# A two-layer graph network behind graph attention: the mix in float32 on four 64x64 blocks of the array, loop written out

## What is computed

```python
u = einsum('bid,bjd->bij', h, h) / sqrt(384)
a = softmax(u, -1)
delta = a * adj
attn = delta / (delta.sum(-1, keepdims=True) + 1e-10)
hl, hs, hr = h @ wl.T + b_l, h @ ws.T + b_s, h @ wr.T + b_r
ctx = (attn * upper) @ hl + diagonal(attn)[..., None] * hs + (attn * lower) @ hr
h = relu((ctx - mean(ctx)) / sqrt(var(ctx) + 1e-12) * g + beta)
```

## Time and profile before

| | us |
|---|---|
| median of 3 runs | 1378.46 (1377.25 to 1379.92) |
| the profiled execution | 1381.73 |
| its span | 1380.0 |
| TensorE busy | 1313.9 |
| VectorE busy | 1057.1 |
| ScalarE busy | 757.1 |
| GpSimd busy | 597.1 |

### The profile page before, as it was taken

One profiled execution on the slowest core, in us unless ns is written; L12 is line 12 of the kernel. 1 busy time (PEld: TensorE's weight loads), 2 busy tenths in 40 slices (PEclk: granted clock), 3 DMA queues, 4 the chain that ended last, 5 costly groups with the idle time before them and its releaser, 6 DMA issues.

```text
span 1380.0 us, 37486 instructions
## 1 busy us (share of the span) xinstructions
PE 1313.9 (95%) x13568; PEld 1289.9 (93%) x13568; DVE 1057.1 (77%) x2665; ACT 757.1 (55%) x1579; POOL 597.1 (43%) x656
## 2 busy tenths in 40 slices
PE   3799999999999999999999999999999999999895
PEld 3799999999999999999999999999999999999884
DVE  3358877878877888887787887788888778787765
ACT  4355555565555565555555555556555556555553
POOL 1344444444444444444444445444444444444432
PEclk9799999999999999999999999999999999999997
DMA  7210111110011111011111011111101111101000
GB/s 243 78 40 2 51 51 52 52 50 19 30 50 50 50 50 40 9 50 50 50 50 50 19 31 50 50 50 50 39 11 50 50 50 50 50 15 26 25 13 24
DMA packets 49445, 62.74 MB, mean 45 GB/s; under 512 B 14320, under 2 KB 35952, under 8 KB 49392
## 3 DMA queue, kind: packets, MB, share of 16 engines
q1 hardware_dynamic: 49392, 62.03, 14.7%
HBM read 36.44 MB, written 12.58 MB: 36 GB/s over the span
## 4 chain that ended last, share of the span: by engine, by line
PE 94%; DMA 2%; issue 1%; DVE 1%; ACT 1%; POOL 0%; SPq 0%; POOLq 0%; ACTq 0%
PE bank L315 26%; PE bank L317 25%; PE bank L316 25%; PE bank L427 4%; PE bank L393 4%; PE bank L378 3%; PE bank L364 3%; PE bank L414 2%; PE bank L404 2%; DMA late<-in_w 2%; PE bank L455 1%; ACT w_hi L520 0%; DVE ln_six L841 0%; DVE w_lo L683 0%; ACT late L621 0%
## 5 line engine op out<-in xcount | busy, mean ns | idle before, releaser
L315 PE MATMUL bank<-w_hi,hT_hi 128*128 128x384 f32 x1152 | 403.0, 350 | 9.6 <-issue 9.2
L316 PE MATMUL bank<-w_lo,hT_hi 128*128 128x384 f32 x1152 | 390.8, 339 | 0.0
L317 PE MATMUL bank<-w_hi,hT_lo 128*128 128x384 f32 x1152 | 390.6, 339 | 0.0
L997 POOL TENSOR_TENSOR hlr_lo<-late,hlr_hi 128x384 fp32r<-128x384 f32 x256 | 240.5, 940 | 245.8 <-ACT hlr_hi L596 244.4
L596 ACT ACTIVATE hlr_hi<-late 128x384 fp32r<-128x384 f32 x256 | 134.5, 526 | 222.3 <-DVE late L798 220.4
L315 PEld LDWEIGHTS bank<-w_hi,hT_hi 128*128 128x128 f32 x1152 | 217.2, 189 | 15.3 <-issue 12.4
L798 DVE TENSOR_TENSOR late<-bank,rows 128x384 f32<-128x384 f32 x256 | 142.1, 555 | 101.9 <-PE bank L317 97.9
L316 PEld LDWEIGHTS bank<-w_lo,hT_hi 128*128 128x128 f32 x1152 | 217.6, 189 | 0.0
L317 PEld LDWEIGHTS bank<-w_hi,hT_lo 128*128 128x128 f32 x1152 | 217.1, 188 | 0.0
L1010 POOL TENSOR_TENSOR ln_rstd<-ln_var,minus_half 128x2 f32<-128x2 f32 x128 | 98.7, 771 | 225.1 <-DVE ln_var L867 117.4
L315 PE MATMUL bank<-xT_hi,w_hi 128*128 128x256 f32 x576 | 164.6, 286 | 8.4 <-ACT kT L535 8.4
(11 more groups left out here) (93 smaller groups left out, 2804.7 us busy)
## 6 DMA issues: line engine op xcount, KB each, us to landing
v_halves<-v_stage SPq DMA_DIRECT2D x128, 99.0 KB, 2.3
xT_in<-in_xT SPq DMA_DIRECT2D x32, 384.0 KB, 3.1
x_in<-in_x SPq DMA_DIRECT2D x32, 384.0 KB, 3.8
out<-late SPq DMA_DIRECT2D x32, 384.0 KB, 2.4
late<-in_w SPq DMA_DIRECT2D x9, 576.0 KB, 6.1
adj_in<-in_adj SPq DMA_DIRECT2D x32, 64.0 KB, 3.5
adjT_in<-in_adjT SPq DMA_DIRECT2D x64, 32.0 KB, 2.9
rows<-in_bl SPq DMA_DIRECT2D x2, 192.0 KB, 6.2
```

Of the source, the lines that this page charges most:

```text
L315: nc.tensor.matmul(o, l_hi, r_hi, start=n == 0, stop=False)
L316: nc.tensor.matmul(o, l_hi, r_lo, start=False, stop=False)
L317: done = nc.tensor.matmul(o, l_lo, r_hi, start=False, stop=n == last)
L997: nc.gpsimd.tensor_tensor(hlr_lo[:, t, m, 0:D], hlr[:, t, m], hlr_hi[:, t, m, 0:D].bitcast(F32), ALU.subtract).then_inc(hlrlo_ready, 1)
```

## The change

The mix isn't split any more: `aT` and `hlr` stay float32, and a product takes one graph of one tile and one side, 64x64 by 386 columns, eight per layer. The first tile's graphs use the diagonal blocks of the array. The second tile's use the other two blocks (`turn`), so that its results come out with the two graphs' partitions exchanged; the second layer exchanges them back. For that the scaled self part of the second tile is written exchanged, in two ScalarE instructions of 64 partitions each, den of the second tile is made in two halves, and the adjacency tiles get a third entry with the second tile's graphs exchanged, which the second layer uses (`entries`). The four split operations of aT and hlr go, and with them their waits. Each engine's steps are all written out, without the loop and the waits that only the loop's form needed.

```diff
 STAGES_BEFORE, STAGES_AFTER = 2, 1
-LOOP_FROM, LOOP_TO = 4, 28
...
+def turn(t, g):
+
+    return g if t == 0 else 1 - g
+
+
+def entries(l):
+
+    return slice(0, T + l, 1 + l)
...
-def steps(nc, engine, emit):
-    for s in range(-STAGES_BEFORE, LOOP_FROM):
-        emit(Step(s // 2, s % 2))
-    with nc.Fori(LOOP_FROM // 2, LOOP_TO // 2, engines=(engine,), hint_back_edge=True) as it:
-        emit(Step(it, 0))
-        emit(Step(it, 1))
-    for s in range(LOOP_TO, UNITS + STAGES_AFTER):
-        emit(Step(s // 2, s % 2))
+def steps(emit):
+    for s in range(-STAGES_BEFORE, UNITS + STAGES_AFTER):
+        emit(Step(s))
...
-        adj_in = sb("adj_in", [P, 2, T, N])
-        adjT_in = sb("adjT_in", [P, 2, T, P])
-        adj_side = sb("adj_side", [P, 2, T, 2, P])
-        adj_diag = sb("adj_diag", [P, 2, T, N])
+
+        adj_in = sb("adj_in", [P, 2, T + 1, N])
+        adjT_in = sb("adjT_in", [P, 2, T + 1, P])
+        adj_side = sb("adj_side", [P, 2, T + 1, 2, P])
+        adj_diag = sb("adj_diag", [P, 2, T + 1, N])
...
-        hlr_hi = sb("hlr_hi", [P, T, 2, MW], F32R)
-        hlr_lo = sb("hlr_lo", [P, T, 2, MW], F32R)
+        hlr = sb("hlr", [P, T, 2, MW])
         aT = sb("aT", [P, T, 2, P])
-        aT_hi = sb("aT_hi", [P, T, 2, P], F32R)
-        aT_lo = sb("aT_lo", [P, T, 2, P], F32R)
-
-        late = sb("late", [P, 10 * D])
-        hlr = late[:, 0:4 * D].rearrange("p (t m d) -> p t m d", t=T, m=2)
-        h_self = late[:, 4 * D:6 * D].rearrange("p (t d) -> p t d", t=T)
-        c0 = late[:, 6 * D:8 * D].rearrange("p (t d) -> p t d", t=T)
-        c1 = late[:, 8 * D:10 * D].rearrange("p (t d) -> p t d", t=T)
+
+        late = sb("late", [P, 9 * D])
+        h_self = late[:, 0:2 * D].rearrange("p (t d) -> p t d", t=T)
+        c0 = late[:, 2 * D:4 * D].rearrange("p (t d) -> p t d", t=T)
+        c1 = late[:, 4 * D:6 * D].rearrange("p (t d) -> p t d", t=T)
+        self_turned = late[:, 6 * D:7 * D]
...
             def mix(st, l):
-                need(pe, aThi_ready, st.count(LATE, 2, l + 1))
-                need(pe, aTlo_ready, st.count(LATE, 2, l + 1))
+
 
                 need(pe, hlr_ready, st.count(LATE, 8, 4 * l + 4))
-                for t in range(T):
-                    need(pe, hlrhi_ready, st.count(LATE, 8, 4 * l + 2 * t + 2))
-                    need(pe, hlrlo_ready, st.count(LATE, 8, 4 * l + 2 * t + 2))
-                    product(CTX_BANKS[t][:, 0:MW],
-                            [((aT_hi[:, t, m, :], aT_lo[:, t, m, :]), (hlr_hi[:, t, m, :], hlr_lo[:, t, m, :]))
-                             for m in (LEFT, RIGHT)]).then_inc(ctx_psum, 1)
+                need(pe, aT_ready, st.count(LATE, 2, l + 1))
+                for m in (LEFT, RIGHT):
+                    for t in range(T):
+                        for g in range(GRAPHS):
+                            rows_of, o = slice(g * N, (g + 1) * N), turn(t, g)
+                            done = nc.tensor.matmul(CTX_BANKS[t][o * N:(o + 1) * N, 0:MW], aT[rows_of, t, m, rows_of],
+                                                    hlr[rows_of, t, m, :], start=m == LEFT, stop=m == RIGHT)
+                        if m == RIGHT:
+                            done.then_inc(ctx_psum, 1)
...
             def scale_self(st, l):
                 need(act, diag_ready, st.count(LATE, 2, l + 1))
-                for t in range(T):
-                    need(act, self_ready, st.count(LATE, 4, 2 * l + t + 1))
-                    nc.scalar.activation(h_self[:, t], h_self[:, t], ACT.Copy,
-                                         scale=diag[:, t:t + 1]).then_inc(self_scaled, 1)
+
+                need(act, ctx_ready[1 - l], st.count(LATE - 1 + l, 2, 2))
+                need(act, self_ready, st.count(LATE, 4, 2 * l + 1))
+                nc.scalar.activation(h_self[:, 0], h_self[:, 0], ACT.Copy, scale=diag[:, 0:1]).then_inc(self_scaled, 1)
+                need(act, self_ready, st.count(LATE, 4, 2 * l + 2))
+                for g in range(GRAPHS):
+                    rows_of, o = slice(g * N, (g + 1) * N), turn(1, g)
+                    nc.scalar.activation(self_turned[o * N:(o + 1) * N], h_self[rows_of, 1], ACT.Copy,
+                                         scale=diag[rows_of, 1:2]).then_inc(self_scaled, 1)
...
-                nc.vector.tensor_tensor(diag_junk[:, :, :], e_di[:, :, 0, :], adj_diag[:, slot], ALU.mult
+                nc.vector.tensor_tensor(diag_junk[:, :, :], e_di[:, :, 0, :], adj_diag[:, slot, entries(l)], ALU.mult
...
             def sides_bias(st, l, t, m):
-                k = 2 * t + m + 1
-                need(dve, hlr_psum, st.count(LATE, 8, 4 * l + k))
-                need(dve, hlrlo_ready, st.count(LATE, 8, 4 * l + k - 4))
-                nc.vector.tensor_tensor(hlr[:, t, m], HLR_BANKS[2 * t + m][:, 0:D], bias_row[l][m], ALU.add
+                need(dve, hlr_psum, st.count(LATE, 8, 4 * l + 2 * t + m + 1))
+
+                need(dve, ctx_psum, st.count(LATE, 4, 2 * l))
+                nc.vector.tensor_tensor(hlr[:, t, m, 0:D], HLR_BANKS[2 * t + m][:, 0:D], bias_row[l][m], ALU.add
                                         ).then_inc(hlr_ready, 1)
 
             def mask_aT(st, l):
                 slot = st.slot(LATE)
+                need(dve, ctx_psum, st.count(LATE, 4, 2 * l))
                 need(dve, eT_psum, st.count(LATE, 2, l + 1))
                 nc.vector.tensor_tensor(aT[:, :, :, :],
                                         AT_BANK[:, 0:T * P].rearrange("p (t i) -> p t i", t=T).unsqueeze(2)
                                         .to_broadcast([P, T, 2, P]),
-                                        adj_side[:, slot], ALU.mult).then_inc(aT_ready, 1)
-
-            def aT_low(st, l):
-                need(dve, aT_ready, st.count(LATE, 2, l + 1))
-                need(dve, aThi_ready, st.count(LATE, 2, l + 1))
-                nc.vector.tensor_tensor(aT_lo[:, :, :, :], aT[:, :, :, :], aT_hi[:, :, :, :].bitcast(F32),
-                                        ALU.subtract).then_inc(aTlo_ready, 1)
+                                        adj_side[:, slot, entries(l)], ALU.mult).then_inc(aT_ready, 1)
...
-                for t in range(T):
-                    need(dve, ctx_psum, st.count(stage, 4, 2 * l + t + 1))
-                    nc.vector.tensor_tensor(den[:, l, t:t + 1], CTX_BANKS[t][:, D:D + 1], dz[:, t:t + 1], ALU.add
+                need(dve, ctx_psum, st.count(stage, 4, 2 * l + 1))
+                nc.vector.tensor_tensor(den[:, l, 0:1], CTX_BANKS[0][:, D:D + 1], dz[:, 0:1], ALU.add
+                                        ).then_inc(den_ready, 1)
+                need(dve, self_scaled, st.count(stage, 6, 3 * l + 1))
+                nc.vector.tensor_tensor(c[l][:, 0], CTX_BANKS[0][:, 0:D], h_self[:, 0], ALU.add
+                                        ).then_inc(ctx_ready[l], 1)
+                need(dve, ctx_psum, st.count(stage, 4, 2 * l + 2))
+                for g in range(GRAPHS):
+                    rows_of, o = slice(g * N, (g + 1) * N), turn(1, g)
+                    turned = slice(o * N, (o + 1) * N)
+                    nc.vector.tensor_tensor(den[turned, l, 1:2], CTX_BANKS[1][turned, D:D + 1], dz[rows_of, 1:2], ALU.add
                                             ).then_inc(den_ready, 1)
-                    need(dve, self_scaled, st.count(stage, 4, 2 * l + t + 1))
-                    nc.vector.tensor_tensor(c[l][:, t], CTX_BANKS[t][:, 0:D], h_self[:, t], ALU.add
-                                            ).then_inc(ctx_ready[l], 1)
+                need(dve, self_scaled, st.count(stage, 6, 3 * l + 3))
+                nc.vector.tensor_tensor(c[l][:, 1], CTX_BANKS[1][:, 0:D], self_turned, ALU.add
+                                        ).then_inc(ctx_ready[l], 1)
 
             def stats_inner(st, stage, l, s_den, s_six, s_mv, s_eps, six, mv, var):
 
-                need(dve, den_ready, st.count(stage, 4, 2 * l + 2))
+                need(dve, den_ready, st.count(stage, 6, 3 * l + 3))
...
-            def sides_low(st, l, t):
-                need(pool, ctx_psum, st.count(LATE, 4, 2 * l + t + 1 - 2))
-                for m in (LEFT, RIGHT):
-                    need(pool, hlrhi_ready, st.count(LATE, 8, 4 * l + 2 * t + m + 1))
-                    nc.gpsimd.tensor_tensor(hlr_lo[:, t, m, 0:D], hlr[:, t, m], hlr_hi[:, t, m, 0:D].bitcast(F32),
-                                            ALU.subtract).then_inc(hlrlo_ready, 1)
...
+    with_turned = lambda a: np.concatenate([a, a[:, 1:2, ::-1]], axis=1)
...
-        "adj": f(adj.reshape(UNITS, T, P, N).transpose(0, 2, 1, 3)),
-        "adjT": f(adj.reshape(UNITS, T, GRAPHS, N, N).transpose(0, 2, 4, 1, 3).reshape(UNITS, P, T, N)),
+        "adj": f(with_turned(adj.reshape(UNITS, T, GRAPHS, N, N)).transpose(0, 2, 3, 1, 4).reshape(UNITS, P, T + 1, N)),
+        "adjT": f(with_turned(adj.reshape(UNITS, T, GRAPHS, N, N)).transpose(0, 2, 4, 1, 3).reshape(UNITS, P, T + 1, N)),
```

(26 more changed lines are left out.)

105 lines of the change are left out of this document (30 added, 75 removed).

## The result

The changed kernel takes 1386.45 us (median of four runs, 1385.69 to 1388.56) where the kernel before takes 1378.72 (with a fourth run beside the three above, 1377.25 to 1379.92): ratio 1.0058, 95% interval 1.0046 to 1.0070. It is 0.6% slower. The profiled execution took 1386.10 us with a span of 1384.4, against 1380.0 before. The granted clock didn't fall: 0.984 of full against 0.982.

What follows compares the result with a forecast made beforehand. TensorE, busy 95% of the span, was taken as the bound, with a chain through xT_lo and score_mask deciding step starts. Terms -4.7 - 16.8 + 16.2 - 1.0 - 0.6 = -6.9 us gave 1372 us; range 1335 to 1390.

Steps and rivals of the forecast that it cites:

- The mix on TensorE: Each layer's mix: 16 records, four blocks at a time, take 1.56 us instead of 2.12, saving 0.56 us per mix.
- Rival (2): Mix on TensorE: only two blocks run at a time, so it takes 2.87 us; 1411 us in all, chance 0.12.
- First layer: First layer's mix: slack ahead of transpose_z covers the saving, so 0.56 us in 30 steps, 16.8 us gained.
- rival (4): First layer: VectorE's long run between the mixes takes the gain back; 1373 to 1389 us, chance 0.11.
- Second layer: Second layer's mix: scaling halves delay xT_lo and the held mask; side projections at T+5.71, not T+5.15; 16.2 us lost.
- small terms: The forecast's smaller amounts, whose bounds alone gave its range of 1363 to 1379 us.
- -16.8 and +16.2: The first layer's mix gain over 30 steps and the second layer's mix loss over 29 steps, in us.
- The loop: Steps written out: all step time in excess of 40.70 us goes, 4.7 us gained.
- Rival (3): Written-out steps: straight code stalls in all 24 steps of the loop, 1.1 us each; 1401 us, chance 0.08.
- The end: Last steps: two transitions without xT_lo gain about 0.5 us each, and the dropped split gains 0.6 in the last step.
- Rival (1): Second layer: VectorE's masks get ahead of xT_lo, step starts at T+4.55, 17 us gained; 1338 us, chance 0.13.

Runs made afterwards that it cites:

- no_turn: The changed kernel without the exchange, so the second tile's graphs use the same two diagonal blocks as the first tile's: 1429.12 us, ratio 1.0362 to the kernel before.
- before_unrolled: The kernel before with its loop written out and the waits only the loop's form needed left away, nothing else: 1375.11 us, ratio 0.9973.
- before_halves: The kernel before, loop written out, with the second tile's h_self scaled in two ScalarE instructions of 64 partitions, in place: 1385.9 us, ratio 1.0053.
- masks_early: The changed kernel with VectorE's score_mask and score_add moved ahead of den and c of the second layer: 1347.56 us, ratio 0.978 to the kernel before.
- masks_between: The changed kernel with xT_hi moved ahead of the second tile's scaling halves and both masks between the two self bias additions: 1338.47 us, ratio 0.9711.
- both_early: The changed kernel with both masks ahead of the second layer's den and c, and xT_hi ahead of the second tile's scaling halves: 1350.0 us, ratio 0.9794.
- after_one_scale: The changed kernel with the second tile's h_self scaled in one 128-partition instruction, without its exchange: 1366.18 us, ratio 0.9914 to the kernel before.

## Why the prediction was wrong

Forecast 1372.0 us, measured 1386.45: it has the wrong sign. The range to 1390 holds it, but only through the rivals' cases; the forecast's own 1363 to 1379 doesn't. By its steps:

- **The mix on TensorE: right.** 1.54 us from T to the transposes, 1.56 predicted, four blocks at a time. The starts of the 16 records of one mix in the trace (ns) are these:

```
718252  718259  718265  718272
718627  718634  718640  718647
718951  718958  718964  718971
719279  719286  719293  719299
```

Four start within 20 ns, and from one four to the next it is 375, 324 and 328 ns; a record was put at 0.33 us. Each four are one record of each of the tiles' four graphs, so four different blocks: in the last four the second and the fourth raise the semaphore of tile 0 and of tile 1, as in the code. Rival (2) falls, and no_turn shows what it would have cost. The rule of the Trainium skill quoted there, "TensorEngine Tiling (Array Packing)", Gotcha 1: PSUM Pressure, isn't borne out in this form: both row halves of a tile write one bank here, in different partitions, and start within 20 ns of each other. Whether two row halves could write the same partitions of a bank at once, no run here shows.

- **First layer: mis-sized.** 0.56 us per step predicted, 0.46 measured. The mix itself is right here too: 733.87 + 0.17 to 735.60 is 1.56 us. What was left out stands behind it: the first value product starts 0.28 us before the next (735.60 to 735.88) where all others have 0.17. I had put 0.1 for leaving the split array into the mix and nothing for this. 0.10 x 30 = 3 us. VectorE didn't take the gain back; rival (4) falls.

- **Second layer: the step that failed.** It is the largest error, 9.3 us of the 15.3 added up below. Mechanism and direction were as predicted: score_mask held until 0.08 us after xT_lo's end, all of TensorE's saving lost and more. The size was not: 0.56 us more predicted, 0.88 measured. Two terms. "I take the latter, less a little, 0.51 us": two halves take 1.28 us and not 1.04, so xT_hi starts at T+2.06 instead of T+1.83 and xT_lo ends at T+4.80 instead of T+4.56: 0.24 us. The upper end was too low: 0.53 us was the distance from a 128-partition scaling to an instruction on another tile, and no row had the new form. From there to the weight load of the side projection 1.23 us instead of 1.15, 0.08 us more: I had taken 0.05 out of 0 to 0.15 for adj_diag beside score_add, and it is 0.13. The trace of the kernel before, with the earlier trace rows, shows where it comes from:

```profile
1167.97 0.45 POOL L977 TENSOR_TENSOR adj_diag<-adj_in,diag_sel 128x128 f32<-128x128 f32 x1
...
1168.12 0.44 DVE L722 SCALAR_TENSOR_TENSOR score_add<-adj_in,beta_col,score_mask 128x128 f32<-128x128 f32 x1
```

score_add is held by adj_diag just as score_mask is by xT_lo: it ends 0.15 us behind adj_diag in both kernels (1168.56 and 1168.42 here, 723.67 and 723.51 in the changed one, rows rounded to 0.01). With the third entry adj_diag has 192 columns and takes 0.59 us instead of 0.45, and the 0.14 us go into the step whole. Together 0.32 x 29 = 9.3 us. VectorE was later than predicted too, score_mask starting at T+3.25 and not T+2.8, but as it is held until xT_lo's end either way, that costs nothing here.

- **The bounds were those of the small terms.** -16.8 and +16.2 stood against each other, and I gave neither an error. 0.15 us per step in each would have been 9 us on either side of 1363 to 1379, up to 1388.

- **The loop: nearly right.** 4.7 us predicted, 3.5 measured in before_unrolled. Rival (3) falls: in the changed kernel steps are 41.13 us from the second on, although its page has 110 packets of instruction fetch (1.80 MB) where the page before has 34 (0.56).

- **The end: mis-sized.** From the start of step 30 on, 2.2 us less was predicted (1.6, and the first layer's 0.56). It is 88.8 us against 89.15 in before_unrolled, 0.35 less. In step 30 TensorE has nothing to do but wait for z, and from T to transpose_z it takes 7.17 us, against 6.97 in before_unrolled, though the mix is 0.6 us shorter. VectorE ends its part behind the mix later: c of the second tile ends at 720.94 + 0.56 = T+3.33 in the timeline above, where it was T+2.95 in the step of the earlier trace rows and the prediction put it at T+2.8. Both tiles' sums are now complete only at the end of the mix, so that the first tile's den starts at T+1.74 (719.91) where it started at T+1.36 (1165.32); and two dens of 64 partitions take 0.34 us, one of 128 takes 0.16.

The errors are 3 + 9.3 + 1.2 + 1.8 = 15.3 us, against 1386.45 - 1372.0 = 14.4.

- **Rival (1) didn't come by itself.** It asked for 0.1 to 0.4 us of luck in the order. score_mask starts 0.27 us behind xT_lo (721.42 and 721.15), and getting it alone ahead isn't enough, as before_halves shows: score_add is held then. What the prediction didn't ask is what it would take to bring the case about. masks_early, one swap, gives 1347.6 us, and masks_between 1338.5, where the rival was priced at 1338.

Open: why an instruction follows a 64-partition scaling only after 0.64 us. adj_diag's share is read from the traces; no run takes it out from beside score_add.

The hold itself agrees with the Trainium skill, "SBUF — State Buffer", its section on who interferes with whom: VectorE and GpSimd share ports by an exclusive lock, and the later one is blocked until the earlier has ended. The same section of the Trainium skill limits this to VectorE instructions in a mode that uses both ports or with two inputs in SBUF. That fits as well: in masks_early hT_lo, one of whose inputs is a bank of PSUM, starts at 701.61 in the middle of xT_lo and takes 1.02 us for both tiles, as elsewhere. In both_early score_mask, started 0.04 us before xT_lo, takes its 0.22 us, and score_add, behind it, 1.78 instead of 0.35; in masks_early, with no GpSimd work beside the masks, neither is held.

## What to carry to other kernels

Before a product is made cheaper, ask what starts the work behind it: here half of the gain could only be had if a mask instruction that waits for nothing of this step came out from behind another engine's long one. An instruction that can be held by GpSimd belongs well ahead of it, by more than its own length and that of the next one that can be held, and not just ahead. Where two such instructions follow each other, each is held by what GpSimd does at its own start, so that the length of even a short GpSimd instruction (adj_diag, 0.59 us) goes into the step. An upper bound for a form of instruction that the trace doesn't show is only as good as the nearest row's likeness: two large terms of opposite sign want their errors added, not their values only.

## What was not expected of the hardware

Rows of the changed kernel by line (busy us, mean ns):

```profile
L582 ACT ACTIVATE late<-late,diag 64x384 f32<-64x384 f32 x128 | 78.5, 613 | 58.4 <-DVE late L779 56.8
...
L578 ACT ACTIVATE late<-late,diag 128x384 f32<-128x384 f32 x64 | 39.4, 616 | 292.9 <-DVE late L779 292.9
```

A ScalarE instruction on 64 partitions takes 613 ns and one on 128 partitions 616, for 384 columns. Behind such a half the next instruction starts 0.64 us after its start, whether it is the other half or xT_hi on another tile (719.59 to 720.23), and also in place and on its own partitions (before_halves), while a 128-partition one is followed by xT_hi after 0.52 to 0.53 us (708.91 to 709.43 in after_one_scale). A mix on four 64x64 blocks costs about 0.1 us on entering it and 0.1 more at the first whole-array product behind it, on top of its records. And the hold is a full one beside short GpSimd instructions too. In every run and every step in which a mask starts beside xT_lo, adj_diag or a select, score_mask ends 0.08 to 0.09 us behind that instruction and score_add 0.14 to 0.15 us, however much of it was left at the start (in one step of the kernel before score_add is held on by the next GpSimd instruction, with the same 0.14 us). So score_add's 0.58 us beside adj_diag (723.09 to 723.67, adj_diag 722.92 to 723.51) instead of 0.35 is not a slower rate, but a wait.
